# First attention of a two-layer language tower: long and short tile rows in turn, head by head

## The chip, the core and the metric

The kernel is one program on one NeuronCore of a Trainium2 chip. The metric is the device time of one execution in microseconds (us). The kernel before took 5799.51 us, the median of three runs (5797.98 to 5799.66).

A core has engines that run side by side, each with its own queue in program order: TensorE (PE: matrix products and transposes, with its weight loads listed as PEld), VectorE (DVE), ScalarE (ACT), GpSimd (POOL) and SyncE (SP, which issues transfers). TensorE writes to PSUM, a small memory in banks; the others read from it and from SBUF. Engines wait for one another by semaphores.

## What is computed

Two layers over 2 sequences of 1024 positions and 1024 channels: a token map, an attention, a feed-forward mixture, a second attention with a top-128 selection, a second mixture. The change concerns the first attention only. Cut to what matters:

```python
# L0 attention: H = 32 heads of 32 channels, 8 groups of key/value heads, so 4 query heads to a group
scores = einsum('bkgtd,bksd->bkgts', Qh, Kh) / sqrt(dh)
scores = where(causal, scores, -inf)
attn   = softmax(scores, axis=-1)
out    = einsum('bkgts,bksd->bkgtd', attn, Vh)
return out.reshape(B, Ts, C) @ Wo
```

## The kernel before, in words

`build` runs seven stages one after the other: `token_map`, `project`, `attention`, `mixture`, `project`, `kept_attention`, `last_mixture`. The change is in `plan`, an inner function of `attention` (lines 536 to 545).

**Tiling.** The 1024 query positions of a sequence are 8 tiles of 128. A *tile row* is one query tile i of one query head m. It is causal, so it has i+1 key tiles: row i = 0 is one tile wide (128 scores for each query), row i = 7 is eight tiles wide (1024). In this text "a row of n tiles" has n = i+1. `PAIRED` (line 525) puts a long row with a short one so that each pair has nine tiles: (7, 0), (6, 1), (5, 2), (4, 3). A *unit* is one such pair for the four heads of one group: 8 tile rows, called steps. Four units make a group (sequence and key/value head), and there are 16 groups, so 64 units and 512 steps. In this text a *cycle* is the four units of one group. The program text holds the eight units of two groups (`STEPS` = 64 steps). `over_pairs` runs it eight times: once written out, six times in a hardware loop, once written out.

**One step s**, by engine:
- `scores(s)` on PE (lines 615 to 627): the products of queries and keys into the slot s % 2 of `ps_s` (two slots of two banks), and at last a product that adds the causal mask (L626). It first waits until the exponential of step s-2, which read the same slot, is done (L620).
- `maxima(s)` on DVE (L743): the negated maximum of each query's scores, into `shift`.
- `exps(s)` on ACT (L701): exp(score + shift) into the slot s % 2 of `prob`, with the sum for each query (a second instruction, ACTIVATION_READ_ACCUMULATOR).
- `turn(s)` on PE (L641): transposes of `prob`, tile by tile, into `ps_t`. `SHARES` cuts a row of more than four tiles into two *chunks*; a shorter one is one chunk. Chunks are numbered through the unit (12 each, `CPU`). Chunk n goes to half n % 2 of `ps_t` and waits until chunk n-2 was copied away (`evacuated`, L629).
- `evac(s)`: the copy of each chunk to `probT`. Chunks of even number are copied by ACT (L712), those of odd number by DVE (L753).

**Once per unit:** `values(u)` on PE (L645): 36 products of transposed probabilities and values into `ps_o` and two transposes of the inverse sums (L661); `invert` on DVE (L758); a widening copy on POOL (L684); `inverse_evac` on ACT (L717); `normalise` on DVE (L764). SP loads a group's queries, keys and values and stores its output.

**The order on each queue** is written out by hand and goes by step number:
- PE, for each s: `turn(s)`, `scores(s+2)`, and after step 1 of a unit `values` of the unit before (lines 668 to 673).
- ACT, for each s: `exps(s+1)`, `evac(s)`, and after step 2 `inverse_evac` (lines 721 to 726).
- DVE, for each s: `maxima(s+1)`, `evac(s)`, after step 0 `invert`, after step 3 `normalise` (lines 771 to 778).

All of these read the unit, the row, the head and the chunk numbers of a step from the one list `PLAN` that `plan` returns. `values` goes by `PAIRED` and by unit, not by step, and `exps` puts its sum in a column that is found from i and m.

Of the kernel before, what the change touches and what calls it, by code (L numbers as in the profile page):

```python
# [26 lines left out]
G = H // HKV  # L27
# [492 lines left out]
def attention(nc, const, qk_dram, v_dram, o_dram):  # L520
# [4 lines left out]
    PAIRED = ((7, 0), (6, 1), (5, 2), (4, 3))  # L525
    UPG = len(PAIRED)
# [9 lines left out]
    def plan():  # L536

        n, steps = 0, []
        for u in range(UNITS):
            for i in PAIRED[u % UPG]:  # L540
                for m in range(G):
                    mine = [(n + c, a, w) for c, (a, w) in enumerate(SHARES[i])]
                    steps.append((u, i, m, mine))
                    n += len(mine)
        return steps

    PLAN = plan()

    with ExitStack() as ctx:
# [1379 lines left out]
```

How the kernel before makes its waits and increments, by code:

```python
            @block.gpsimd  # L128
            def _(pool):
                pool.dma_start(idx[:, :], ids).then_inc(ids_in, 16)
                pool.wait_ge(ids_in, 16)
                for j in range(NT):
                    nc.gpsimd.indirect_dma_start(
                        out=rows[:, j, :], out_offset=None, in_=embedding,
                        in_offset=bass.IndirectOffsetOnAxis(ap=idx[:, j:j + 1].bitcast(U32), axis=0),
                    ).then_inc(rows_in, 16)
# [1 line left out]
            @block.sync  # L138
            def _(sp):
                sp.dma_start(ident[:, :], const["ident"]).then_inc(const_in, 16)
                sp.dma_start(cmat[:, :], compat).then_inc(const_in, 16)
                for j in range(NT):
                    sp.wait_ge(h_ready, j + 1)
                    sp.dma_start(h_dram[j * P:(j + 1) * P, :], hout[:, j % 4, :]).then_inc(stored[j % 4], 16)
                for k in range(4):
                    sp.wait_ge(stored[k], 16 * (NT // 4))
# [1 line left out]
            @block.vector  # L148
            def _(dve):
                dve.wait_ge(rows_in, 16 * NT)
                nc.vector.tensor_reduce(top[:, :], rows[:, :, :], AX_X, ALU.max)
                dve.drain()
                nc.vector.tensor_tensor(prob[:, :, :], rows[:, :, :], top[:, :].unsqueeze(2).to_broadcast([P, NT, C]),
                                        ALU.subtract).then_inc(shifted, 1)
                dve.wait_ge(exped, 1)
                nc.vector.tensor_reduce(total[:, :], rows[:, :, :], AX_X, ALU.add)
```

## Time and profile before

| | us |
|---|---|
| median of three runs | 5799.51 |
| the profiled execution, whole | 5802.05 |
| its span (first to last instruction) | 5800.2 |
| first attention, first to last exponential (L701) | 527.6 to 1472.8 |
| PE busy, whole span | 3975.3 |
| DVE busy, whole span | 3821.2 |
| ACT busy, whole span | 3315.8 |
| mean granted clock of TensorE, share of 2.4 GHz | 0.847 |

A group or an event of the trace names the line of the code, the engine, the operation, what is written and read, and how often (x). An "idle before" in brackets is the time for which the engine sat idle just before, with what ended it. "issue" there is a wait for nothing that the profile shows. The seven stages follow each other, so the attention's time counts in full towards the whole.

### The profile page before, as it was taken

How to read it: one execution, taken by the hardware profiler on the slowest of the kernel's cores; microseconds unless marked ns; L12 is line 12 of the kernel's file. 1: busy time of each engine (PE TensorE's matmuls, PEld its weight loads, DVE VectorE, ACT ScalarE, POOL GpSimd, SP SyncE). 2: the span in 40 equal slices, each digit the busy share in tenths (PEclk: the TensorE clock that was granted, in tenths of full speed). 3: DMA queues.
4: the chain of work that ended last, by engine and by line, in shares of the span. 5: the costliest groups of instructions: out<-in, count | busy, mean ns of one | idle time of the engine just before them, and what ended most of it. 6: DMA issues, size and time to landing. Idle time of an engine off the chain costs nothing. (4 is left out here: it accounts for less than half of the span.)

```text
span 5800.2 us, 80523 instructions
## 1 busy us (share of the span) xinstructions
PE 3975.3 (69%) x23480; PEld 2373.9 (41%) x23480; DVE 3821.2 (66%) x10794; ACT 3315.8 (57%) x7698; POOL 289.1 (5%) x213
## 2 busy tenths in 40 slices
PE   6997888888899989814555545555455554554599
PEld 2444555555444444402333323333233332333354
DVE  1663666666233346458888888888888888888443
ACT  1113666666100011168888888888888888888200
POOL 1331000000000023300000000000000000000000
PEclk7998999999999999956777777777777777777799
DMA  3223222212311132310011010110101100010222
GB/s 122 68 68 70 61 56 48 69 47 50 113 44 43 43 101 68 72 30 21 4 24 23 21 23 4 23 23 21 22 5 23 23 21 17 10 23 5 69 66 80
DMA packets 277680, 250.19 MB, mean 43 GB/s; under 512 B 169968, under 2 KB 210048, under 8 KB 277248
## 3 DMA queue, kind: packets, MB, share of 16 engines
q1 hardware_dynamic: 276704, 245.60, 16.2%
q14 instruction: 313, 2.56, 0.2%
q8 instruction: 119, 1.95, 0.1%
q0 software_dynamic: 544, 0.07, 0.0%
HBM read 168.03 MB, written 77.59 MB: 42 GB/s over the span
## 5 line engine op out<-in xcount | busy, mean ns | idle before, releaser
L1013 ACT ACTIVATE a_sign<-a_x,a_state 128x256 fp8e4<-128x256 f32 (+6 forms) x2240 | 1833.7, 820 | 393.6 <-DVE a_state L1134 254.0
L922 PE MATMUL a_ps_s<-a_k,a_q 128*128 128x512 bf16 (+3 forms) x1536 | 479.5, 454 | 749.6 <-DVE a_x L1241 709.4
L950 PE MATMUL a_ps_o<-a_probT,a_v 128*32 128x128 f32 x4608 | 649.2, 289 | 461.8 <-ACT a_probT L983 457.1
L950 PEld LDWEIGHTS a_ps_o<-a_probT,a_v 128*32 128x32 f32 x4608 | 483.6, 115 | 597.3 <-ACT a_probT L983 548.9
L322 PE MATMUL p_ps_qkv<-p_w,p_hT 128*128 128x512 f32 x1536 | 676.6, 597 | 3.3 <-ACT p_hT L360 2.3
L701 ACT ACTIVATE a_prob<-a_ps_s,a_shift 128x640 f32<-128x640 f32 (+7 forms) x512 | 379.9, 742 | 349.0 <-DVE a_shift L743 304.0
L922 PEld LDWEIGHTS a_ps_s<-a_k,a_q 128*128 128x128 bf16 x1536 | 153.8, 123 | 986.6 <-DVE a_x L1241 809.6
L641 PE MATMUL a_ps_t<-a_ident,a_prob 128*128 128x128 f32 x2304 | 369.3, 286 | 164.8 <-ACT a_prob L701 100.9
L743 DVE TENSOR_REDUCE a_shift<-a_ps_s 128x1 f32<-128x640 f32 (+7 forms) x512 | 384.3, 753 | 111.2 <-PE a_ps_s L626 105.2
L322 PEld LDWEIGHTS p_ps_qkv<-p_w,p_hT 128*128 128x128 f32 x1536 | 289.1, 191 | 348.0 <-issue 344.9
L1145 DVE TENSOR_SCALAR_CACHE_REDUCE a_above<-a_x,a_state 128x256 bf16<-128x256 f32 (+3 forms) x448 | 391.8, 875 | 47.3 <-issue 38.2
L1013 ACT ACTIVATION_READ_ACCUMULATOR a_sign<-a_x,a_state 128x1 f32 x2240 | 422.8, 189 | 0.0
L1241 DVE TENSOR_SCALAR_CACHE_REDUCE a_x<-a_ps_s 128x128 f32<-128x128 f32 (+7 forms) x512 | 368.6, 756 | 65.2 <-issue 35.5
L933 PE MATMUL a_ps_t<-a_ident,a_prob 128*128 128x128 f32 x2304 | 409.8, 314 | 0.0
L983 ACT COPY a_probT<-a_ps_t 128x512 f32<-128x512 f32 (+3 forms) x768 | 349.9, 471 | 79.6 <-PE a_ps_t L933 78.9
L1150 DVE MAX8 a_nine<-a_below 128x8 f32<-128x256 f32 (+3 forms) x448 | 371.1, 828 | 33.0
L1231 DVE SCALAR_TENSOR_TENSOR a_prob<-a_x,a_limit,a_prob 128x256 f32<-128x256 f32 (+6 forms) x448 | 380.5, 881 | 10.5 <-issue 3.7
L753 DVE COPY a_probT<-a_ps_t 128x384 f32<-128x384 f32 (+3 forms) x384 | 222.0, 578 | 248.7 <-PE a_ps_t L641 245.2
L1147 DVE SCALAR_TENSOR_TENSOR a_below<-a_above,a_x 128x256 f32<-128x256 bf16 (+3 forms) x448 | 363.3, 811 | 7.2
L641 PEld LDWEIGHTS a_ps_t<-a_ident,a_prob 128*128 128x128 f32 x2304 | 252.3, 142 | 269.1 <-ACT a_prob L701 98.3
L623 PE MATMUL a_ps_s<-a_k,a_q 128*128 128x512 bf16 (+3 forms) x1536 | 339.9, 331 | 23.4 <-DMA a_v<-v 23.4
L1025 ACT ACTIVATE a_prob<-a_x,a_shift 128x256 f32<-128x256 f32 (+6 forms) x448 | 331.2, 813 | 0.0
(200 smaller groups left out, 5292.3 us busy)
## 6 DMA issues: line engine op xcount, KB each, us to landing
a_q<-qk SPq DMA_DIRECT2D x256, 256.0 KB, 4.9
qk<-p_qkT SPq DMA_DIRECT2D x32, 960.0 KB, 6.2
p_h<-h SPq DMA_DIRECT2D x32, 512.0 KB, 7.0
a_k<-qk SPq DMA_DIRECT2D x256, 64.0 KB, 5.1
m_o<-o SPq DMA_DIRECT2D x32, 512.0 KB, 5.4
m_h<-h SPq DMA_DIRECT2D x32, 512.0 KB, 5.5
p_w<-in_wqkv SPq DMA_DIRECT2D x16, 768.0 KB, 12.5
h<-tok_h SPq DMA_DIRECT2D x16, 512.0 KB, 2.6
```

Of the source, the lines that this page charges most:

```text
L322: m = nc.tensor.matmul(ps_qkv[:, n * BANK:(n + 1) * BANK], hT[:, par, k * P:(k + 1) * P], w[:, k, n * BANK:(n + 1) * BANK], start=(k == 0) ...
L641: mm = nc.tensor.transpose(ps_t[:, n % 2, c * P:(c + 1) * P], prob[:, s % 2, (a + c) * P:(a + c + 1) * P], ident[:, :])
L701: nc.scalar.activation(prob[:, s % 2, 0:w], ps_s[:, s % 2, 0:w], ACT.Exp, bias=shift[:, s % 4:s % 4 + 1], accum_out=total[:, u % 2, j:j + ...
L743: nc.vector.tensor_reduce(shift[:, c:c + 1], ps_s[:, s % 2, 0:(i + 1) * P], AX_X, ALU.max, negate=True).then_inc(shift_ready, 1)
L922: nc.tensor.matmul(ps_s[:, n % 2, a:a + w], q[:, y, head, i * P:(i + 1) * P], k[:, y, a:a + w], start=(y == 0), stop=False, skip_group_che ...
L933: mm = nc.tensor.transpose(ps_t[:, (n + 1) % 3, c:c + P], prob[:, par, at:at + P], ident[:, :])
L950: mm = nc.tensor.matmul(ps_o[strip:strip + DH, c:c + P], v[:, b * DH:(b + 1) * DH], probT[:, n % 2, b * P:(b + 1) * P], start=(b == 0), st ...
L1013: ins = nc.scalar.activation(sign[:, off(i):off(i) + w], x[:, par, at:at + w], ACT.Sign, scale=-1.0, saturate=False, bias=state[:, par, 0, ...
L1145: lambda: nc.vector.tensor_scalar(above[:, r, 0:w], x[:, y, at:at + w], tl, None, ALU.is_ge, ALU.add, accum_out=exact[:, n:n + 1]),
L1150: lambda: nc.vector.max(nine[:, n, 1:9], below[:, r, 0:w]),
L1231: nc.vector.scalar_tensor_tensor(out=prob[:, y, at:at + w], in0=x[:, y, at:at + w], scalar=limit[:, r:r + 1], in1=prob[:, y, at:at + w], o ...
L1241: nc.vector.tensor_scalar(x[:, y, at:at + w], ps_s[:, n % 2, 0:w], 1.0, None, ALU.mult, ALU.max, accum_out=top[:, y, n:n + 1]).then_inc(x_ ...
```

## The change

The two inner loops of `plan` change places. Within a unit the steps were: the long row of heads 0, 1, 2, 3, then the short row of heads 0, 1, 2, 3. Now they are: long and short row of head 0, long and short row of head 1, and so on. Numbers of steps, chunks and instructions stay. What follows from the numbering:
- even steps are long rows, odd steps short ones, so slot 0 of `ps_s` and of `prob` holds long rows only, and slot 1 short rows only;
- chunks are numbered in the new order: the long row of head 0 has chunks 0 and 1, its short row 2; head 1 has 3, 4 and 5; head 2 has 6, 7 and 8; head 3 has 9, 10 and 11. Before, they were 0 to 7 for the long rows and 8 to 11 for the short ones. So heads 1 and 3 now have the first chunk of the long row copied by DVE and the second by ACT.

```diff
         for u in range(UNITS):
-            for i in PAIRED[u % UPG]:
-                for m in range(G):
+            for m in range(G):
+                for i in PAIRED[u % UPG]:
                     mine = [(n + c, a, w) for c, (a, w) in enumerate(SHARES[i])]
                     steps.append((u, i, m, mine))
                     n += len(mine)
```

## Rows read from the trace of the kernel before

**Rows 1.** Busy time by stretch, the first attention: us, busy of each engine, PEclk, DMA.

```profile
524.00:1476.00 952.00, 786.04 (x9043) 562.20 (x9047) 603.28 (x1023) 582.25 (x1471) 25.77 (x64) 0.99 0.23 53
```

**Rows 2.** Timeline of ACT, one cycle (start us, us, ...): exponentials of steps 0 and 2.

```profile
821.82 1.11 ACT L701 ACTIVATE a_prob<-a_ps_s,a_shift 128x1024 f32<-128x1024 f32 x1 [1.09 <-DVE a_shift L743]
...
826.53 1.11 ACT L701 ACTIVATE a_prob<-a_ps_s,a_shift 128x1024 f32<-128x1024 f32 x1 [1.23 <-PE a_ps_t L641]
...
836.93 1.01 ACT L701 ACTIVATE a_prob<-a_ps_s,a_shift 128x896 f32<-128x896 f32 x1 [1.31 <-DVE a_shift L743]
...
841.19 1.01 ACT L701 ACTIVATE a_prob<-a_ps_s,a_shift 128x896 f32<-128x896 f32 x1 [1.52 <-DVE a_shift L743]
...
851.31 0.90 ACT L701 ACTIVATE a_prob<-a_ps_s,a_shift 128x768 f32<-128x768 f32 x1 [0.81 <-DVE a_shift L743]
...
855.11 0.90 ACT L701 ACTIVATE a_prob<-a_ps_s,a_shift 128x768 f32<-128x768 f32 x1 [1.17 <-DVE a_shift L743]
...
865.37 0.80 ACT L701 ACTIVATE a_prob<-a_ps_s,a_shift 128x640 f32<-128x640 f32 x1 [0.48 <-DVE a_shift L743]
...
868.72 0.80 ACT L701 ACTIVATE a_prob<-a_ps_s,a_shift 128x640 f32<-128x640 f32 x1 [0.88 <-PE a_ps_t L641]
...
880.38 1.11 ACT L701 ACTIVATE a_prob<-a_ps_s,a_shift 128x1024 f32<-128x1024 f32 x1 [1.09 <-DVE a_shift L743]
```

**Rows 3.** Timeline, unit (6, 1): from the exponential of step 0 to that of step 2.

```profile
837.84 0.19 ACT L701 ACTIVATION_READ_ACCUMULATOR a_prob<-a_ps_s,a_shift 128x1 f32 x1
...
838.16 0.98 PE L641 MATMUL a_ps_t<-a_ident,a_prob 128*128 128x128 f32 x7 [1.46 <-ACT a_prob L701]
...
839.73 0.75 PEld L641 LDWEIGHTS a_ps_t<-a_ident,a_prob 128*128 128x128 f32 x7
...
839.99 1.09 DVE L743 TENSOR_REDUCE a_shift<-a_ps_s 128x1 f32<-128x896 f32 x1
```

**Rows 4.** Groups by line and shape: widest and five-tile maxima and exponentials, one copy.

```profile
L743 DVE TENSOR_REDUCE a_shift<-a_ps_s 128x1 f32<-128x1024 f32 x64 | 78.2, 1223 | 43.6 <-PE a_ps_s L626 42.5
L701 ACT ACTIVATE a_prob<-a_ps_s,a_shift 128x1024 f32<-128x1024 f32 x64 | 71.3, 1115 | 92.6 <-DVE a_shift L743 75.7 <-PE a_ps_t L641 8.6 <-issue 8.2
...
L712 ACT COPY a_probT<-a_ps_t 128x512 f32<-128x512 f32 x96 | 55.5, 578 | 5.7 <-PE a_ps_t L641 5.7
L743 DVE TENSOR_REDUCE a_shift<-a_ps_s 128x1 f32<-128x640 f32 x64 | 52.8, 824 | 13.0 <-PE a_ps_s L626 12.3
L701 ACT ACTIVATE a_prob<-a_ps_s,a_shift 128x640 f32<-128x640 f32 x64 | 50.9, 795 | 34.3 <-DVE a_shift L743 23.8 <-PE a_ps_t L641 10.5
```

**Rows 5.** Timeline of PEld, unit (6, 1): from the start of values to the next transposes.

```profile
841.46 1.90 PEld L655 LDWEIGHTS a_ps_o<-a_probT,a_v 128*32 128x32 f32 x72 [0.21 <-issue]
...
843.73 0.80 PEld L641 LDWEIGHTS a_ps_t<-a_ident,a_prob 128*128 128x128 f32 x7
```

**Rows 6.** Timeline of PEld: scores of a two-tile row, up to the next transposes.

```profile
844.50 0.21 PEld L623 LDWEIGHTS a_ps_s<-a_k,a_q 128*128 128x128 bf16 x2
...
844.71 0.10 PEld L626 LDWEIGHTS a_ps_s<-a_bias_b,a_ident_b 128*128 128x128 bf16 x1
...
844.90 0.31 PEld L641 LDWEIGHTS a_ps_t<-a_ident,a_prob 128*128 128x128 f32 x3
```

**Rows 7.** Waits of PE in the first attention: us in total, times, longest.

```profile
PE a_ps_s L623 <- DMA a_v<-v: 23.4, 1, 23.4
PE a_ps_t L641 <- issue: 12.0, 5, 2.6
```

**Rows 8.** Busy time by stretch, after one loop top and between two: columns as in group 1.

```profile
884.10:887.50 3.40, 3.40 (x14) 2.27 (x13) 2.42 (x4) 1.65 (x4) 0.40 (x1) 0.50 0.00 0
...
890.00:1000.00 110.00, 91.22 (x1050) 65.03 (x1040) 70.02 (x122) 68.04 (x177) 2.82 (x7) 1.00 0.26 61
```

**Rows 9.** Timeline of PE at a loop top: eight-tile transposes of steps 0 and 1.

```profile
882.70 1.09 PE L641 MATMUL a_ps_t<-a_ident,a_prob 128*128 128x128 f32 x8 [2.26 <-issue]
...
884.99 1.91 PE L641 MATMUL a_ps_t<-a_ident,a_prob 128*128 128x128 f32 x8
```

## The prediction, made before the changed kernel was run

> **What bounds the kernel now.** I read the busy time of the stretch first, then the timeline of one cycle, then the waits of PE. In the first attention PE is listed busy for 786 of 952 us, DVE for 603, ACT for 582 [rows 1]. None is full, so the question is what each waits for. The timeline of a unit gives it [rows 2, 3]. The exponential of step 0 in unit (6, 1) starts at 836.93 and its sum is out at 837.84 + 0.19 = 838.03. PE starts to transpose it 0.13 us later, at 838.16. It puts the scores of step 2 behind that and is free at 839.73, so transposes and scores of a seven-tile row take 1.57 us of PE's queue. The maximum of step 2 starts at 839.99 and ends at 841.08, and the exponential of step 2 starts at 841.19. This is a closed loop without slack: exponential, transposes, scores, maximum, exponential, all through one slot of the scores. It takes 841.19 - 836.93 = 4.26 us. The two slots carry two such loops side by side, and before the change each slot holds two long and two short rows of a unit.
>
> The same distance from step 0 to step 2 is the loop of each long row [rows 2]: 4.71 us for eight tiles (826.53 - 821.82), 4.26 for seven, 3.80 for six (855.11 - 851.31), 3.35 for five (868.72 - 865.37). I take this cycle, which doesn't begin at a loop top, for all 16. The cycle as a whole takes 880.38 - 821.82 = 58.56 us.
>
> **The change, part by part.** No instruction is added or removed. What moves is the order, and with it which slot a row uses. Long rows have even steps now, so all four long rows of a unit go through slot 0, one after the other, and the short ones through slot 1. The wait that decides is an old one: scores of step s+2 wait for the exponential of step s. Step s+2 of a long row is now the next head's long row.
>
> *The chain of slot 0.* From one long exponential to the next it is: exponential and transposes of the old row, then scores and maximum of the new one. Summed over a whole cycle each long row gives its own loop once for each head: 4 x (4.71 + 4.26 + 3.80 + 3.35) = 4 x 16.12 = 64.48 us, against 58.56 now. So +5.92 us a cycle.
>
> *What the short rows cost beside it.* Their exponential runs while PE transposes the long row, their maximum while ACT has the long exponential, their transposes and scores on PE behind the long scores, where PE is idle. That idle stretch, from PE being free after the long scores to the next long transposes, is the loop less the 1.57 us: 4.26 - 1.57 = 2.69 us for seven tiles. It is nearly all maximum and exponential, which grow by (1.223 - 0.824 + 1.115 - 0.795) / 3 = 0.24 us a tile [rows 4]. So it is 2.93, 2.69, 2.45 and 2.21 us for eight to five tiles. Short transposes take 0.107 us each (seven in 0.75 [rows 3]). Short scores take 0.40 us for two tiles (844.90 - 844.50 [rows 6]); seven tiles take 1.57 - 0.75 = 0.82, so 0.084 a tile, and I take 0.32, 0.40, 0.48 and 0.57 for one to four. Together 0.43, 0.61, 0.80 and 1.00 us for the short rows of one to four tiles, which fit. Cost: nothing. If an engine were busy then, the long row would wait for the difference.
>
> *Values.* Once a unit PE has 843.73 - 841.46 = 2.27 us of values [rows 5], right behind the short scores of head 1. PE idles 0.21 us ahead of them [rows 5]; 0.09 of that lies behind any short scores (844.71 + 0.10 to 844.90 [rows 6]) and is counted, 0.12 is not. Now the transposes of the long row of head 1 are queued behind the values. In the idle stretch PE has 0.43 + 2.39 = 2.82 of 2.93 us to do in unit (7, 0), 3.00 of 2.69 in (6, 1), 3.19 of 2.45 in (5, 2), 3.39 of 2.21 in (4, 3). The excess goes onto the chain: 0 + 0.31 + 0.74 + 1.18 = 2.23 us a cycle. The bounds are 0, if values fit in after all, and 3.0, if each sum is 0.2 us short; I take 2.23, since every part has a row.
>
> *Chunks.* The second chunk of the long row of heads 1 and 3 waits for ACT's copy of the short row before, and ACT does that copy behind the long exponential. In unit (4, 3) the copy of four tiles takes 0.578 us [rows 4] while the first chunk, two transposes, takes 0.21 us after a start at 0.13: some 0.2 us are exposed, twice, 0.4 us a cycle. In the other units the short copy is smaller and the first chunk longer, and it is hidden.
>
> *Loop tops.* At five of them PE idles for "issue", 12.0 us in all [rows 7], as the code jumps back. Now the jump falls behind the short scores of the next unit's head 0, where PE is idle for over 2.4 us anyway. So I give back 12 us (bounds: 0 and 12). Transfers: PE waited for one once, at the stage's start [rows 7]; a slower stage gives SP more time.
>
> *The clock of TensorE.* After each loop top the granted clock is 0.50, that is 1.2 GHz, for a few us; in the 110 us between two it is 1.00, that is 2.4 GHz [rows 8]. What came ahead was a pause of PE of 2.26 us (884.1 follows 882.70 [rows 9]); the pause of 1.46 us in unit (6, 1) [rows 3], which each cycle has, was followed by no fall. After the change unit (7, 0) has three pauses of about 2.93 - 0.43 = 2.5 us (the fourth is filled by values), (6, 1) three of about 2.1, the others shorter ones. At the low clock eight transposes take 1.91 in place of 1.09 us [rows 9], +0.82; if the scores double with them, +1.85 in all for a step. So 16 x 3 = 48 pauses in units (7, 0) cost from 0 to 48 x 1.85 = 89 us. Between these ends I take a fall at half of them, since the pauses are about as long as those at the loop tops but a fall stretches PE's work in the loop that follows, and 1.2 us for each, as part of a step is done before the fall: +29 us.
>
> *Sum.* 16 x (5.92 + 2.23 + 0.4) = 137, less 12, plus 29: +154 us. The profiled execution took 5802.05 us (span 5800.2 and 1.85 around it), 2.5 us over the median; 5956 there, 5953 on the median's scale.
>
> **A rule that speaks the other way.** The rows show two regimes, long rows at 4.26 us for two and short ones, and no engine full in either. The Trainium skill, Perfetto Trace Analysis, Optimization Strategy, says that where the most-contended engine changes over time, performance may be improved by interleaving the regimes, which is what this edit does. By that rule the time would fall, as in the second rival below. No row here shows an interleaved stretch of this stage.
>
> **Rivals.**
> - *The clock holds, or falls everywhere.* Without falls the sum is +125 us, 5924 us; with a fall at each of the 48 pauses +214, 6013 us. For the first speaks that pauses come and go with full work between them, as the 1.46 us pauses do; for the second that these are as long as those at the loop tops and come three in a row.
> - *Interleaving fills the queues (faster).* If the long scores did not have to wait for the long exponential before them, PE's queue would decide: in unit (6, 1) 4 x 1.57 + 4 x 0.61 + 2.39 = 11.1 us against 851.31 - 836.93 = 14.4 now [rows 2, 3, 5, 6]. That is 3.3 us a unit, 64 units, -211 us: 5589 us. It decides as soon as the long loop comes under the mean of 58.56 / 16 = 3.66 us a pair that the kernel has now; the mean loop is 4.03. Against it: PE's 1.46 us pause in rows 3 ends with that very exponential, and the wait stands in the code.
> - *A draw.* The long loop would be 0.4 us shorter on average when its neighbour is short, because its exponential or maximum now queues behind something. In rows 3 each step follows its forerunner by 0.11 to 0.26 us, which leaves nothing to shorten. It gives 5800 us.
> - *The change does less than it says.* All engines read the same list, so the order cannot change on one alone; I give this nothing.
>
> **How the numbers follow.** Forecast, with the clock falling at some of the pauses: 0.55. Clock holding: 0.25. Falling everywhere: 0.12. Draw: 0.03. Faster: 0.05. No change means within 0.2%, 12 us, about what a measurement of this kernel can tell. Slower: 0.55 + 0.25 + 0.12 = 0.92. The range reaches from 5885 us (no fall, and values at 0 in place of 2.23: 16 x 6.32 - 12 = +89 us, rounded down) to 6015 us (a fall at each pause, rounded up). It leaves out the draw and the faster case, 0.08, and some 0.1 for terms that I have missed.
>
> **What would show it.** Right: exponentials of long rows 4.7, 4.3, 3.8 and 3.4 us apart in one unit, each ended by its maximum, with the short exponential between; PE's waits for the exponential (L641 behind L701) larger and without "issue"; a cycle of 66 to 69 us; stretches at a granted clock of 0.50 inside units (7, 0). Wrong: long exponentials of neighbouring heads closer than 4 us in unit (7, 0), or a stage that ends before 1580 us.

## The result and the profile after

The changed kernel took 5975.37 us (median of four runs, 5967.43 to 5979.41) against 5799.59: a ratio of 1.0303, 95% interval 1.0287 to 1.0320, so 176 us slower. The profiled execution took 5967.43 us, the shortest of the four and 165.4 more than that of before. The first attention, from its first exponential to the end of its last, runs from 529.3 to 1640.2 us, 1110.9 us in place of 945.3. All of the loss, +165.6 us, lies in this stage.

Busy time by stretch over the stage, columns as in [rows 1]:

```profile
529.00:1641.00 1112.00, 801.49 (x9006) 585.45 (x9006) 594.63 (x1021) 587.14 (x1471) 25.36 (x63) 0.93 0.19 45
```

PE, DVE and ACT do the work that they did before (PE is listed busy for 15 us more, as part of its work now runs at the low clock); the stretch is longer by waiting. The granted clock is 0.93 in the mean, where it was 0.99 [rows 1]. It has two levels, 1.00 and 0.50; the stretches at 0.50, that is 1.2 GHz, add up to 148 us, in 37 falls, where they were 22 us in 5.

Timeline of ACT, the long exponentials only: unit (7, 0), then units (5, 2) and (4, 3) of the same cycle, then a unit (6, 1):

```profile
735.87 1.11 ACT L701 ACTIVATE a_prob<-a_ps_s,a_shift 128x1024 f32<-128x1024 f32 x1 [1.70 <-DVE a_shift L743]
...
740.59 1.12 ACT L701 ACTIVATE a_prob<-a_ps_s,a_shift 128x1024 f32<-128x1024 f32 x1 [2.11 <-DVE a_shift L743]
...
745.16 1.11 ACT L701 ACTIVATE a_prob<-a_ps_s,a_shift 128x1024 f32<-128x1024 f32 x1 [1.32 <-DVE a_shift L743]
...
749.88 1.11 ACT L701 ACTIVATE a_prob<-a_ps_s,a_shift 128x1024 f32<-128x1024 f32 x1 [2.11 <-DVE a_shift L743]
...
754.20 1.01 ACT L701 ACTIVATE a_prob<-a_ps_s,a_shift 128x896 f32<-128x896 f32 x1 [1.35 <-DVE a_shift L743]
...
773.84 0.90 ACT L701 ACTIVATE a_prob<-a_ps_s,a_shift 128x768 f32<-128x768 f32 x1 [1.11 <-DVE a_shift L743]
...
777.64 0.90 ACT L701 ACTIVATE a_prob<-a_ps_s,a_shift 128x768 f32<-128x768 f32 x1 [1.62 <-DVE a_shift L743]
...
782.11 0.90 ACT L701 ACTIVATE a_prob<-a_ps_s,a_shift 128x768 f32<-128x768 f32 x1 [0.94 <-DVE a_shift L743]
...
789.37 0.79 ACT L701 ACTIVATE a_prob<-a_ps_s,a_shift 128x640 f32<-128x640 f32 x1 [0.98 <-DVE a_shift L743]
...
792.72 0.80 ACT L701 ACTIVATE a_prob<-a_ps_s,a_shift 128x640 f32<-128x640 f32 x1 [1.17 <-DVE a_shift L743]
...
797.26 0.79 ACT L701 ACTIVATE a_prob<-a_ps_s,a_shift 128x640 f32<-128x640 f32 x1 [0.70 <-DVE a_shift L743]
...
804.79 1.11 ACT L701 ACTIVATE a_prob<-a_ps_s,a_shift 128x1024 f32<-128x1024 f32 x1 [1.70 <-DVE a_shift L743]
...
828.03 1.01 ACT L701 ACTIVATE a_prob<-a_ps_s,a_shift 128x896 f32<-128x896 f32 x1 [2.14 <-DVE a_shift L743]
...
844.90 0.90 ACT L701 ACTIVATE a_prob<-a_ps_s,a_shift 128x768 f32<-128x768 f32 x1 [1.11 <-DVE a_shift L743]
```

Each ends a wait for its maximum. From one row to the next in unit (7, 0) it is 4.72, 4.57, 4.72 and 4.32 us: the loop that [rows 2] shows for one pair of long rows, now four times in a row. Units (7, 0) and (6, 1) are picked without a fall of the clock (1.00 in the mean of both), the other two never had one. They take 754.20 - 735.87 = 18.33, 844.90 - 828.03 = 16.87, 789.37 - 773.84 = 15.53 and 804.79 - 789.37 = 15.42 us: 66.15 us for a cycle without falls, against 58.56 [rows 2]. The second distance in a unit shows values: 782.11 - 777.64 = 4.47 where the first is 3.80, and 797.26 - 792.72 = 4.54 where it is 3.35.

Timeline of one loop, from the end of a long exponential to the start of the next at 749.88 (compare [rows 3]):

```profile
746.17 0.19 ACT L701 ACTIVATION_READ_ACCUMULATOR a_prob<-a_ps_s,a_shift 128x1 f32 x1
...
746.49 1.09 PE L641 MATMUL a_ps_t<-a_ident,a_prob 128*128 128x128 f32 x8 [2.35 <-ACT a_prob L701]
...
748.54 1.42 DVE L743 TENSOR_REDUCE a_shift<-a_ps_s 128x1 f32<-128x1024 f32 x2 [0.23 <-PE a_ps_s L626]
```

PE idles 2.35 us, starts 0.13 us after the sum is out (746.36), and DVE starts the long maximum as the scores end. The short maximum is merged into the same DVE row and comes after it. Waits of PE in the stage; the first was 100.9 us, 140 times, before:

```profile
PE a_ps_t L641 <- ACT a_prob L701: 305.0, 194, 2.6
...
PE a_ps_t L641 <- ACT a_probT L712: 5.6, 16, 0.4
```

What a fall of the clock does stands in a unit (6, 1), timeline of PE, and in the granted clock (third column from the end) of the stretch beside it:

```profile
755.43 1.26 PE L641 MATMUL a_ps_t<-a_ident,a_prob 128*128 128x128 f32 x7 [2.00 <-ACT a_prob L701]
756.49 1.70 PE L623 MATMUL a_ps_s<-a_k,a_q 128*128 128x512 bf16 x4
```

```profile
755.90:759.30 3.40, 3.40 (x19) 1.99 (x21) 1.77 (x3) 0.48 (x1) 0.40 (x1) 0.51 1.06 214
```

After a pause of 2.00 us the clock is at 1.2 GHz. The scores, 0.92 us in the same unit at the full clock, take 1.70, and the loop takes 759.53 - 754.20 = 5.33 us in place of 4.26. Summed over the units of the trace, what goes beyond the clean unit is 35 us in units (7, 0), of which 21 in the five at loop tops, 23 us in units (6, 1), and nothing in the others. Of the 37 falls 26 lie in units (7, 0) and 11 in units (6, 1).

### The profile page after: what moved, and what is told of

The parts are those of the page before. It is cut to its first block and busy times, and to the rows that moved or that the text cites. A ratio compares the mean times of both kernels' runs of the same rounds, so it can differ in the third digit from the quotient of the medians.

```text
span 5965.6 us, 80619 instructions
## 1 busy us (share of the span) xinstructions
PE 3991.2 (67%) x23480; PEld 2396.4 (40%) x23480; DVE 3814.3 (64%) x10794; ACT 3320.7 (56%) x7698; POOL 289.1 (5%) x213
## 5 line engine op out<-in xcount | busy, mean ns | idle before, releaser
L922 PE MATMUL a_ps_s<-a_k,a_q 128*128 128x512 bf16 (+3 forms) x1536 | 475.2, 450 | 752.8 <-DVE a_x L1241 712.8
L701 ACT ACTIVATE a_prob<-a_ps_s,a_shift 128x1024 f32<-128x1024 f32 (+7 forms) x512 | 379.9, 743 | 444.0 <-DVE a_shift L743 430.9
L641 PE MATMUL a_ps_t<-a_ident,a_prob 128*128 128x128 f32 x2304 | 375.6, 291 | 311.2 <-ACT a_prob L701 305.0
L743 DVE TENSOR_REDUCE a_shift<-a_ps_s 128x1 f32<-128x1024 f32 (+7 forms) x512 | 377.8, 754 | 152.7 <-PE a_ps_s L626 146.7
L623 PE MATMUL a_ps_s<-a_k,a_q 128*128 128x512 bf16 (+3 forms) x1536 | 372.8, 356 | 23.4 <-DMA a_v<-v 23.4
```

The costliest lines, as they stand in the source:

```text
L623: nc.tensor.matmul(ps_s[:, s % 2, a:a + w], q[:, x, y, m, i * P:(i + 1) * P], k[:, x, y, a:a + w], start=(y == 0), stop=False, skip_group_ ...
L641: mm = nc.tensor.transpose(ps_t[:, n % 2, c * P:(c + 1) * P], prob[:, s % 2, (a + c) * P:(a + c + 1) * P], ident[:, :])
L701: nc.scalar.activation(prob[:, s % 2, 0:w], ps_s[:, s % 2, 0:w], ACT.Exp, bias=shift[:, s % 4:s % 4 + 1], accum_out=total[:, u % 2, j:j + ...
L743: nc.vector.tensor_reduce(shift[:, c:c + 1], ps_s[:, s % 2, 0:(i + 1) * P], AX_X, ALU.max, negate=True).then_inc(shift_ready, 1)
L922: nc.tensor.matmul(ps_s[:, n % 2, a:a + w], q[:, y, head, i * P:(i + 1) * P], k[:, y, a:a + w], start=(y == 0), stop=False, skip_group_che ...
```

## The experiments

Times are medians; the kernel before, run again beside each group of runs, had medians of 5796.34 to 5800.52. Three edits recur. **Bank**: the output tile gets one PSUM bank in place of two, which frees one (values then wait for `normalise` of the unit just before; PE's waits in run 5 show none for it). **Slots**: with that bank, long rows use the two old slots by head, short rows the new bank. **Orders**: on PE scores(s+2) goes ahead of turn(s), on DVE maxima(s+2) ahead of evac(s).

**1. Only the late units in turn.**

```diff
-            for m in range(G):
-                for i in PAIRED[u % UPG]:
+            pair = PAIRED[u % UPG]
+            turns = [(i, m) for i in pair for m in range(G)] if u % UPG < 2 else [(i, m) for m in range(G) for i in pair]
+            for i, m in turns:
...
```

> Long and short rows in turn only in units (5, 2) and (4, 3); units (7, 0) and (6, 1) keep the old order. Theory (chain of long rows in one slot, plus the clock in units with long pauses): from the two profiles these two units take 15.53 + 15.42 us in turn against 14.06 + 15.01 before, so +1.9 us a cycle, 16 cycles, +30 us over the kernel before, about 5830 us, and no stretch at the low clock but those after the five loop tops. Rival (turning the order costs the same wherever it is done): about half of the whole loss, +88 us, 5888 us.

Measured: 5820.38 against 5797.87, ratio 1.0037 (1.0023 to 1.0051), +22.5 us. The clock of the stage is 1.00. Timeline of ACT, long exponentials: the first two of a unit (5, 2), then the first of the two units behind it:

```profile
859.83 0.90 ACT L702 ACTIVATE a_prob<-a_ps_s,a_shift 128x768 f32<-128x768 f32 x1 [0.80 <-DVE a_shift L744]
...
863.63 0.90 ACT L702 ACTIVATE a_prob<-a_ps_s,a_shift 128x768 f32<-128x768 f32 x1 [1.62 <-DVE a_shift L744]
...
875.36 0.79 ACT L702 ACTIVATE a_prob<-a_ps_s,a_shift 128x640 f32<-128x640 f32 x1 [0.98 <-DVE a_shift L744]
...
890.78 1.11 ACT L702 ACTIVATE a_prob<-a_ps_s,a_shift 128x1024 f32<-128x1024 f32 x1 [1.70 <-DVE a_shift L744]
```

The two units take 15.53 and 15.42 us, as in the changed kernel, and a cycle away from a loop top 60.43, 1.87 over [rows 2], which is 30 us for 16. At loop tops a cycle takes 0.9 us more, where it took 2.4 more before; five times 1.5 is the 7 us that are missing from the 30. The expectation had left the falls of the clock at the loop tops in; they are gone too. The loss goes by the length of the rows; the rival is out.

**2. Only the early units in turn.** The same diff with `u % UPG >= 2`.

> The complement of the first run: long and short rows in turn only in units (7, 0) and (6, 1). Theory: the parts add. Without falls of the clock these two units take 18.33 + 16.86 us in turn against 15.11 + 14.38 before, +5.7 us a cycle, +91 us; less 12 at the loop tops; and nearly all of the clock's 58 us lie here: +137 us, 5935 us within 15. Rival (the clock falls only because all units have pauses): no stretch at 0.50 beyond the loop tops, 5875 to 5885.

Measured: 5948.98 against 5796.55, ratio 1.0268 (1.0250 to 1.0286), +152 us. With the 22.5 of the run above that is 175 of 176: the parts add, though this one came out 14 us over the forecast. The clock of the stage is 0.93, as in the changed kernel, so its falls belong to units (7, 0) and (6, 1).

**3. PE's pauses filled.** With *Bank*; the products have no reader.

```diff
+                        if s % SPU in (3, 5, 7):
+                            for _ in range((12, 8, 0, 0)[s // SPU % UPG]):
+                                nc.tensor.matmul(ps_x[:, 0:P], ident_b[:, :], bias_b[:, :], start=True, stop=True,
+                                                 skip_group_check=True)
```

> The changed kernel with idle products of 128 columns on PE in its pauses (12 behind the short scores of steps 3, 5 and 7 of units (7, 0), 8 in units (6, 1)), into a bank of their own, which is had by giving the output one bank in place of two. Theory: the low clock costs some 58 us of the loss; the stretches at 0.50 inside units go, and the time falls by 45 to 60 us to about 5920. Rival (the low stretches lie beside other work and cost nothing; the loss is all chain): no change, 5975, or slower by what the products take.

Measured: 5924.39 against 5797.87, ratio 1.0216 (1.0199 to 1.0233), 51 us less than the changed kernel, with 960 products more (60 in each of 16 cycles) that nobody reads. By the profiled executions it is 42 us, 36 of them in this stage: 22 in units (6, 1), which are clean now, and 13 in units (7, 0). The stage:

```profile
527.00:1602.00 1075.00, 803.90 (x9835) 620.13 (x9962) 593.67 (x1019) 585.69 (x1469) 25.21 (x63) 0.98 0.20 46
```

So the low clock is a cause of its own, beside the chain; *Bank* alone was not run, but it stands in run 5 too, which changed nothing. The Trainium skill, TensorE: Matmul & The Clock Gate, Part 1, says that the array is throttled by default and activity releases it; the trace agrees, 0.93 without the products and 0.98 with them.

**4. One more pause filled**, the one ahead of unit (7, 0): `(12, 8, 0, 12 if s % SPU == 7 else 0)`.

> The run with idle products once more, with 12 products also behind step 7 of units (4, 3), the pause ahead of the first long row of unit (7, 0), which was left open there and after which 12 stretches at the low clock stayed. Theory: they go, and with them about 1.1 us each, 13 us: 5911 us, within 6, and the mean clock of the stage is 1.00. Rival (the loop tops or the switch of unit bring the falls, not the pause): 5924.

Measured: 5926.35, ratio 1.0224 (1.0206 to 1.0242); no gain. Away from loop tops the falls are gone, but for one in the first cycle, and cycles take 66.15 us, the clean cycle. In a filled pause PE still idles, and the clock holds (0.99 in the mean of the stage). But at the five loop tops PE waits for "issue" again, as in [rows 7]. Timeline and waits of PE:

```profile
873.52 1.09 PE L642 MATMUL a_ps_t<-a_ident,a_prob 128*128 128x128 f32 x8 [1.68 <-ACT a_prob L706]
```

```profile
PE a_ps_t L642 <- issue: 16.7, 5, 3.7
```

In the profiled executions units (7, 0) gave back 9 us away from the loop tops and lost 5 at them, so the stage is 4 us shorter (1071.2 in place of 1075.3). The whole isn't, as the stages behind it took 5 us more; in the profiled executions of all these kernels these take 4321 to 4329 us, though nothing in them was changed. So the forecast of 13 us failed on a cost that I had not priced, at the jump back. Whether it is the 12 products ahead of the jump or the longer code that costs there, no run shows.

**5. The third slot alone.** *Bank* and *Slots*:

```diff
-                        wait_met(pe, exp_done, at(STEPS, s - 1))
+                        wait_met(pe, exp_done, at(STEPS, s - 1 if i < 4 else s - 3))
...
-                                nc.tensor.matmul(ps_s[:, s % 2, a:a + w], q[:, x, y, m, i * P:(i + 1) * P],
+                                nc.tensor.matmul(slot(i, m, a, a + w), q[:, x, y, m, i * P:(i + 1) * P],
```

> The changed kernel with three slots for scores: long rows by turns in the two old ones, short rows in a bank of their own; the output has one bank in place of two. Orders stay. Theory: scores of the next long row need not wait for the exponential any more, but they stand behind the transposes on PE, which wait for the same exponential, so nothing changes: 5975 us, within 0.3%. Rival (the wait for the slot is the whole cause): the long rows run at PE's pace and the time falls below 5800.

Measured: 5973.30, ratio 1.0300 (1.0283 to 1.0317), no change. PE's wait for the exponential is about what it was, 305.0:

```profile
PE a_ps_t L646 <- ACT a_prob L706: 302.6, 192, 2.9
```

The Trainium skill, Perfetto Trace Analysis, Optimization Strategy, says that a gap that repeats can mean too few buffers. A buffer more gave nothing here, because the wait also stands in the queue, at the transposes ahead of the scores (run 8 shows it).

**6. The orders alone.** *Orders*:

```diff
-                        turn(s)
                         if s + 2 < STEPS or not last:
                             scores(s + 2)
+                        turn(s)
...
-                        if s + 1 < STEPS or not last:
-                            maxima(s + 1)
+                        if s + 2 < STEPS or not last:
+                            maxima(s + 2)
```

> The changed kernel with two orders changed: on PE scores(s+2) ahead of turn(s), on DVE maxima(s+2) ahead of evac(s). The slots stay. Theory (closed loop exponential, transposes, scores, maximum): the transposes leave the loop, so the long loops become 3.86, 3.51, 3.16 and 2.81 us, 53.4 us a cycle; values then stick out by some 4.9 us a cycle; the pauses shrink below 1.7 us and the clock holds. About 58.3 us a cycle against 66.1 and 58 us of clock back: 5790 us, within 30. Rival (an engine's queue bounds the pair, not the loop): no change beyond the clock's share, 5915 to 5975.

Measured: 5815.59, ratio 1.0031 (1.0019 to 1.0044), 160 us less than the changed kernel. Steps 0 and 2 of a unit (6, 1) on ACT, and PE at the scores of that step 0:

```profile
843.82 1.01 ACT L701 ACTIVATE a_prob<-a_ps_s,a_shift 128x896 f32<-128x896 f32 x1
...
847.21 1.01 ACT L701 ACTIVATE a_prob<-a_ps_s,a_shift 128x896 f32<-128x896 f32 x1 [0.39 <-DVE a_shift L743]
```

```profile
841.44 0.93 PE L623 MATMUL a_ps_s<-a_k,a_q 128*128 128x512 bf16 x4 [1.19 <-ACT a_prob L701]
```

The loop is 3.39 us, 0.87 less than 4.26; the transposes' 0.75 have left it. PE still waits for the exponential, now with the scores. A cycle takes 58.67 us, as forecast (58.3); the 26 us over the forecast are the five loop tops, 5.3 us each. The orders on PE and on DVE were not tried one without the other.

**7. The old order of rows with the orders**, the same diff on the kernel before.

> The kernel before, with the old order of rows, and scores(s+2) on PE ahead of turn(s), maxima(s+2) on DVE ahead of evac(s). Theory: each slot holds two long and two short rows of a unit, and each loses its transposes from the loop: 2 x 0.75 + 2 x 0.2 = 1.9 us a unit in (6, 1), some of it given back because values cover them: about 1.4 us a unit, 64 units, less 15 to 27 us at the loop tops: 5720 us, within 40. So the two orders of rows differ by some 95 us with scores taken ahead (5816 in turn), as by 176 without. Rival (with scores ahead the order of rows no longer matters): 5816.

Measured: 5714.15 against 5796.34, ratio 0.9853 (0.9836 to 0.9869): faster than the kernel before, and 101 us below run 6. A cycle takes 53.14 us. So the order of rows matters as long as a slot's loop decides, by the long rows that share the slot.

**8. Slots and orders together.**

> The changed order of rows with both: three slots for scores as in the run of the slots alone, and scores and maxima taken ahead as in the run of the orders alone. Theory: slot and queue order are two locks on the same loop; with both open the loop is gone and PE's queue decides. Unit (6, 1): 4 x 1.57 + 4 x 0.61 + 2.39 = 11.1 us; about 11.5 us a unit, 64 units, and some 5 us at each of five loop tops: 5630 us, within 50, faster than the kernel before. Rival (the slots are of no consequence once the orders are right): 5816, as with the orders alone.

Measured: 5707.79, ratio 0.9845 (0.9829 to 0.9862). 108 us come off run 6, so both locks were real, but the forecast of 5630 was too low: a cycle takes 52.16 us. The pair at values takes 5.2 us, the others 2.1 to 3.4. PE at values and DVE's next long maximum:

```profile
904.30 2.17 PE L660 MATMUL a_ps_o<-a_probT,a_v 128*32 128x128 f32 x72
...
907.80 1.23 DVE L748 TENSOR_REDUCE a_shift<-a_ps_s 128x1 f32<-128x1024 f32 x1 [2.75 <-PE a_ps_s L631]
```

DVE idles 2.75 us, as the next scores stand behind values. A loop top costs 4.8 us here, 1.6 in run 7.

**9. Values in halves, in the changed kernel.** Five of the nine key tiles behind step 1, four with the inverse sums behind step 3:

```diff
+                                done += 1
+                                if done // 5 != part:
+                                    continue
...
-                            values(s // SPU - 1)
+                            values(s // SPU - 1, 0)
+                        if s % SPU == 3 and not (first and s < SPU):
+                            values(s // SPU - 1, 1)
```

> The changed kernel with the values of a unit in two halves, five of the nine key tiles behind step 1 and four with the inverse sums behind step 3 (the copy of the inverse sums and the last product on ACT and DVE moved by two steps). Theory: values stick out of the pause of PE by 1.9 us a cycle (4.47 against 4.26, 4.47 against 3.80, 4.54 against 3.35 us in the three units); in halves they fit all but 0.1, so 16 x 1.8 = 29 us come back, and two pauses of each unit (7, 0) and (6, 1) are half filled, so less time at the low clock, 10 to 30 us: 5915 to 5940 us. Rival (what sticks out is not PE's work but the wait for the copies of the last chunks): no gain, 5975.

Measured: 5923.28, ratio 1.0217 (1.0199 to 1.0234), 52 us less. The second distances in units (5, 2) and (4, 3) are 3.70 and 3.46 us in place of 4.47 and 4.54. That is 22 us for these units. The profiled executions, the changed kernel's shortest and this one's longest, differ by 37 us, nearly all of it in the stage: beside the 22, 14 us in units (6, 1), and nothing in units (7, 0). The clock stays at 0.93.

**10. Slots, orders and values in halves.**

> Three slots, scores and maxima ahead, and values in halves. Theory: PE's queue already decides without halving, and halving does not change its work; 0 to 30 us below the run with slots and orders alone, about 5610 us. Rival (values stop the long rows there too, since ACT and DVE run dry behind them): 40 us or more below it.

Measured: 5720.93, ratio 0.9871 (0.9854 to 0.9887), 13 us slower than run 8. Neither theory forecast that. The trace shows where it lies: both pairs that hold a half are slowed, 3.73 and 4.58 us in unit (7, 0), where run 8 has 5.13 at values and 2.93 behind it. Why two halves cost more than the whole stays open.

**11. Slots and orders, scores of step 4 ahead of values.** Against run 8:

```diff
-                        if s + 2 < STEPS or not last:
+                        early = not (first and s < SPU)
+                        if not (s % SPU == 2 and early) and (s + 2 < STEPS or not last):
                             scores(s + 2)
                         turn(s)
-                        if s % SPU == 1 and not (first and s < SPU):
+                        if s % SPU == 1 and early:
+                            scores(s + 3)
                             values(s // SPU - 1)
```

> Three slots, scores and maxima ahead, and at step 1 of a unit the scores of step 4 also issued ahead of values (5.2 us a pair there in the run of slots and orders, 2.6 to 2.9 in the others, since DVE and ACT run dry behind values). Theory: DVE has a maximum to take while PE works on values, so that pair falls to about 3.7 us; 64 x 1.5 = 96 us below 5708: about 5612 us, within 40. Rival (PE's queue itself is full there): 5708.

Measured: 5683.27, ratio 0.9804 (0.9787 to 0.9822), 25 us less where 96 were expected. The maximum now runs beside values, but the exponential behind it doesn't:

```profile
921.60 2.17 PE L660 MATMUL a_ps_o<-a_probT,a_v 128*32 128x128 f32 x72
921.71 0.96 DVE L750 TENSOR_REDUCE a_shift<-a_ps_s 128x1 f32<-128x768 f32 x1 [0.23 <-PE a_ps_s L631]
...
923.98 0.82 PE L646 MATMUL a_ps_t<-a_ident,a_prob 128*128 128x128 f32 x6
```

The maximum is out at 922.67, its exponential starts at 925.48: it needs the slot of `prob` whose transposes stand behind values and end at 924.80. Two copies stand ahead of it on ACT too (`evac` from 924.84, `inverse_evac` from 925.21), and both need what PE does at or behind values.

**12. Slots and orders, values behind step 2**, with scores(s + 3) ahead of them there, and the last two steps of the output moved by two.

> Three slots, scores and maxima ahead, and values behind step 2 of a unit (behind the transposes of the long row of head 1), with the scores of step 5 issued ahead of them; the copy of the inverse sums and the last product moved by two steps. In the run before (scores of step 4 ahead of values) the pair at values still took 4.9 us, because the exponential of step 4 needs the slot of prob whose transposes stood behind values. Theory: that was the last lock; the pair falls to about 3.5 us, 45 to 47 us a cycle in place of 50.5: 5615 us, within 30. Rival (PE's queue is full there): 5683, no change.

Measured: 5673.11 us, the lowest of all; ratio to its own runs of before 0.9758 (0.9679 to 0.9837), an interval made wide by one run of before that took 5870.40 us. The forecast of 5615 failed again: the pair at values takes 4.5 to 4.9 us and a cycle 49.9, 10 us below run 11 in all, and what holds that pair was not followed up. PE's queue is nearly full now, 759 of 820 us, which neither the kernel before (786 of 952, [rows 1]) nor the changed one had:

```profile
529.00:1349.00 820.00, 759.13 (x9004) 553.34 (x9002) 577.91 (x1021) 582.05 (x1471) 25.36 (x63) 0.98 0.26 61
```

## Why the prediction was right

5953 us was forecast, 5975 measured, inside 5885 to 6015. By its steps, in the profiled execution (+165 there, +154 forecast):

- **The chain of slot 0** was forecast at +5.92 us a cycle, by the first distance of each unit. Without falls a cycle takes 66.15 us; less values (2.51) and chunks (0.35) that is 63.29, +4.7. The 1.2 us less are hand-offs. In the clean units the first and third distances have 0.13 us from the sum to the transposes and 0.11 from the maximum to the exponential. The last ones have 0.05 and 0.03 (in unit (7, 0) from 751.08 to 751.13 and from 754.17 to 754.20), and so does the second in unit (7, 0), where values fit in: 4.57 in place of 4.72, 0.15 us less, twice in each of four units. The mechanism is shown from both sides: runs 1 and 2 add up by row length, and runs 5, 6 and 8 open the loop. It has two locks, the slot and PE's queue order, of which the prediction named the first; in turn, the time falls below that of before only with both open.
- **The short rows cost nothing**: right; the first distances in the four units, 4.72, 4.26, 3.80 and 3.35 us, are those of [rows 2] to 0.01.
- **Values** were forecast at 0, 0.31, 0.74 and 1.18 us for the four units. The second distance less the first or third gives -0.15, 0.21, 0.66 and 1.19; with the 0.15 of the shorter hand-offs that is 0, 0.36, 0.81 and 1.34, 2.51 in place of 2.23. Behind values the transposes start 0.05, 0.46, 0.92 and 1.45 us after the sum is out. Run 9 removes most of it.
- **Chunks**: 0.4 us a cycle were forecast, twice 0.2. The wait row has 5.6 us in 16 times: 0.35 us once a cycle. For head 1 values hide it.
- **Loop tops**: the old 12 us went, but not without a trace. At the first loop top PE idles 2.74 us for issue (PEld), and the transposes of step 0 start at 806.67, 0.55 us late (the sum is out at 805.99):

```profile
805.80 0.19 ACT L701 ACTIVATION_READ_ACCUMULATOR a_prob<-a_ps_s,a_shift 128x1 f32 x1
806.67 1.12 PEld L641 LDWEIGHTS a_ps_t<-a_ident,a_prob 128*128 128x128 f32 x8 [2.74 <-issue]
```

  I had counted "over 2.4 us" of idle time there, but PE first transposes a short row of four tiles, and without the jump the pause would be only 2.2 (from 803.93, where PEld falls idle, to 806.12).
- **The clock** is the term that was mis-sized: +29 us forecast with bounds of 0 and 89. What the units take beyond the clean ones is 58 us, with what the loop tops add. Run 3 still loses 10 us at its five loop tops and run 4 16; if they cost as much here, 42 to 48 us are the clock's. I had put 24 falls, at half of the pauses, in units (7, 0) alone. There it was near: 26 came. What I had wrong is the pauses of units (6, 1), which brought 11 falls more and cost 23 us: a fall stands behind all six pauses of 1.92 to 2.00 us there, and behind 5 of the 27 of 1.8 to 1.9.
- **The sum** was forecast as 137 for chain, values and chunks, less 12, plus 29. Found were 16 x (66.15 - 58.56) = 121, less the 12 that the old loop tops had cost, plus 58 for clock and new loop tops: 167. The terms missed by -16 and +29 and partly cancel, so the total came out better than its parts; that much is luck. Of the signs named, the cycle of 66 to 69 us holds only away from loop tops (65.9 to 69.6 and one of 71.5); at them it is 70.9 to 72.6.
- **The rule that spoke the other way** (the Trainium skill, Perfetto Trace Analysis, Optimization Strategy: interleave regimes) did not hold by itself, at 1.0303. With slots and orders opened the turn of rows gives 5708 us (run 8), the old order with the orders alone 5714 (run 7). Their runs overlap (5706.26 to 5711.72, 5706.70 to 5715.28), and run 8 has a third slot that run 7 lacks: a cycle is 1 us shorter in run 8, and its loop tops give most of that back. So no gain from interleaving is shown here. The old order with a third slot was not run.

## What to carry to other kernels

With two buffers taken in turn, what shares a buffer matters as much as what stands next in the queue: put long and short items into each buffer, or the long ones form one chain. Before adding a buffer, look which wait stands first in the queue; here the buffer alone gained nothing, and with the queue order changed it gained 108 us. And price PE's pauses: here a chain that left PE idle for some 2 us at a time also cost the clock.

## What the runs showed of the hardware

- Work that nobody reads made the kernel faster: 12 or 8 products of 128 columns in a pause raised the clock of the stage from 0.93 to 0.98 and took 51 us off (run 3).
- What a loop top added to its cycle differed from run to run: 2.4 us for each of five before, with a fall of the clock behind it, 0.9 us in run 1, without one, 5.3 us with the orders (run 6), and nothing visible in run 2, where cycles at a loop top took 68.0 us and the others, with falls of their own, 68.6.
- The same hand-off between two engines took one of two times, by turns: in unit (7, 0) of the changed kernel 0.13 or 0.05 us from ACT's sum to PE's transposes, and 0.11 or 0.03 from DVE's maximum to ACT's exponential. Why, no run shows.
- The changed kernel's four runs spread by 12 us (5967 to 5979), and those of runs 2, 5 and 9, whose stage has the same low clock (0.92 to 0.93), by 14, 10 and 9; those of before shown beside the changed kernel spread by 5.
